# Selective-scan and attention kernel: directions joined without a drain, B and C rows loaded apart, first job's operands loaded a stretch ahead

## What is computed

```python
def step(h, xs_t):                       # over L = 2304 positions
    d_t, u_t, B_t, C_t = xs_t
    dA = jnp.exp(d_t[..., None] * A)     # 192 channels x 16 states
    h = h * dA + (d_t * u_t)[..., None] * B_t[:, :, None, :]
    y = jnp.einsum('bkdn,bkn->bkd', h, C_t)
    return (h, y)
...
xs = jnp.stack([x_hw, x_wh, x_hw[..., ::-1], x_wh[..., ::-1]], axis=1)   # 4 directions
delta = jax.nn.softplus(dts + dt_b[None, :, :, None])
...
ys = ys[:, 0:2] + ys[:, 2:4, :, ::-1]    # directions 0 and 2, 1 and 3 are added
```

## Time and profile before

| what | value |
|---|---|
| runs | 10106.07, 10117.13, 10135.11 us |
| profiled execution, span of the program on the core | 10102.8 us |
| median of the runs over that span | 14.3 us more |
| busy share of the span | PE 78%, DVE 72%, ACT 64%, POOL 60% |
| scans | 2304 (8 images x 288 steps) |
| DMA | 1534.77 MB, mean 152 GB/s |

### The profile page before, as it was taken

The page is one execution under the profiler, slowest core; times in us unless marked ns, Lnnn a source line. Parts: engine busy times, 40 slices in busy tenths (PEclk is TensorE's granted clock), DMA queues, the critical chain, the costliest instruction groups (busy, mean ns, idle before and its releaser), DMA issues.

```text
span 10102.8 us, 176447 instructions
## 1 busy us (share of the span) xinstructions
PE 7866.5 (78%) x54736; PEld 2569.1 (25%) x54736; DVE 7322.5 (72%) x6576; ACT 6466.3 (64%) x11830; POOL 6076.6 (60%) x4450
## 2 busy tenths in 40 slices
PE   5576668888788887888778887888878884888768
PEld 2122222222222232222322222222222221222212
DVE  1788848886688866888488875888668895889620
ACT  2343348775577746777477764877468783777578
POOL 0677627774477735777267763877448783777310
PEclk7565579897898978998788987988789995989789
DMA  2556525654356625565256552565345652565300
GB/s 62 165 182 196 182 72 185 190 187 126 123 187 186 186 86 165 186 187 175 74 185 191 186 162 87 187 192 181 113 137 187 193 184 79 187 189 181 109 27 20
DMA packets 767149, 1534.77 MB, mean 152 GB/s; under 512 B 85304, under 2 KB 411428, under 8 KB 757232
## 3 DMA queue, kind: packets, MB, share of 16 engines
q1 hardware_dynamic: 761584, 1520.71, 48.2%
q10 hardware_dynamic: 4608, 2.36, 0.1%
HBM read 1270.29 MB, written 252.44 MB: 151 GB/s over the span
## 4 chain that ended last, share of the span: by engine, by line
PE 37%; issue 19%; DVE 14%; ACT 11%; DMA 9%; POOL 5%; SPq 4%; ACTq 1%; DVEq 0%; POOLq 0%
PE ps L1896 7%; DMA job_u<-u_scratch 6%; PE ps L1828 6%; PE ps L1762 5%; PE ps L1816 5%; ACT probs_buf L1251 4%; DVE rings L1478 4%; DVE ps L1457 3%; DVE job_buf L1478 3%; POOL hc_buf L1016 2%; PE ps L1803 2%; PE ps L1845 1%; PE ps L2012 1%; ACT rings L1238 1%; PE ps L2011 1%
## 5 line engine op out<-in xcount | busy, mean ns | idle before, releaser
L1251 ACT ACTIVATE probs_buf<-ps 128x384 f32<-128x384 f32 x6912 | 3151.0, 491 | 1168.1 <-PE ps L1896 1102.9
L1016 POOL TENSOR_TENSOR hc_buf<-rings,rep 128x768 f32<-128x768 f32 x1152 | 2094.0, 1818 | 1220.6 <-DVE rings L1478 794.6
L1896 PE MATMUL ps<-qp_buf,kp_buf 108*128 108x384 bf16 x6912 | 2282.3, 351 | 616.4 <-ACT probs_buf L1251 283.2
L1016 POOL TENSOR_TENSOR hc_buf<-job_buf,rep 128x768 f32<-128x768 f32 x1152 | 2094.8, 1818 | 979.1 <-DVE job_buf L1478 970.1
L1457 DVE TENSOR_TENSOR ps<-ps,rep 128x768 f32<-128x768 f32 x2304 | 2175.9, 944 | 506.6 <-PE ps L1804 383.3
L1828 PE MATMUL ps<-probs_buf,v_buf 128*13 128x384 f32 x13824 | 1571.1, 529 | 75.0 <-DVE att_buf L1496 43.9
L1816 PE MATMUL ps<-hc_buf,sum_states 128*32 128x144 f32 x24576 | 1496.8, 331 | 145.0 <-POOL hc_buf L1016 111.3
L1803 PE MATMUL ps<-st_buf,pick_channel 96*128 96x512 bf16 x2304 | 1005.5, 436 | 588.4 <-DVE rings L1478 231.0
L1478 DVE TENSOR_TENSOR_SCAN job_buf<-rings,ps 128x768 f32<-128x768 f32 x768 | 1368.4, 1782 | 100.5 <-ACT rings L1238 55.2
L1896 PEld LDWEIGHTS ps<-qp_buf,kp_buf 108*128 108x128 bf16 x6912 | 648.5, 97 | 3087.2 <-ACT probs_buf L1251 2132.5
L1238 ACT ACTIVATE st_buf<-st_buf,a_cols 128x768 f32<-128x768 f32 x1152 | 1062.2, 927 | 88.0 <-DMA st_buf<-delta_scratch 87.8
(11 more groups left out here) (196 smaller groups left out, 7851.1 us busy)
## 6 DMA issues: line engine op xcount, KB each, us to landing
st_buf<-delta_scratch SPq DMA_DIRECT2D x1152, 384.0 KB
rings<-delta_scratch SPq DMA_DIRECT2D x1152, 384.0 KB
part_scratch<-job_buf SPq DMA_DIRECT2D x1152, 72.0 KB, 3.2
st_buf<-part_scratch SPq DMA_DIRECT2D x192, 432.0 KB, 6.9
rep<-xd_scratch SPq DMA_DIRECT2D x192, 384.0 KB
job_u<-u_scratch SPq DMA_DIRECT2D x192, 192.0 KB
delta_scratch<-job_buf SPq DMA_DIRECT2D x192, 192.0 KB, 4.8
qp_buf<-qk_scratch SPq DMA_DIRECT2D x864, 36.0 KB
```

The source lines that it names most:

```text
L1016: pool.tensor_tensor(hc[tile % 2][:, chunk(kk, v)], h_ring[t % 2], rep_third(1, kk, v), ALU.mult).then_inc(s["hc_ready"], 1)
L1251: act.activation(probs[(m % 2) * HG + h], bank(slots["score", p]), ACT.Exp, scale=SCALE)\
L1896: pe.matmul(bank(slots["score", p]), k_parts[:, h, m * 128:(m + 1) * 128], q_ring[:, (kk * NS + q) % 2, h, :], start=True, stop=True).then ...
```

## The change

Four things are changed.

1. The six sum parts and two evacuations at the end of a direction are taken into the next direction's first steps, where the same steps of any other stretch do them for the stretch before. This holds for the three joins of an image. The last direction still ends with them.
2. `y_stored` becomes one semaphore for each q. The y of stretch 5 is no longer stored in a row of 16 DMAs right after it, but over t = 5 to 8 of stretch 6. Direction 2 waits for `y_stored[q]` before it overwrites that part of `y_acc`, at t = 6 of each stretch.
3. Chunks 1 and 2 of B are loaded in steps 22 and 23 of the last stretch, as `b_ready` tells that DVE has finished with the old third. C chunk 1 is loaded in step 23, and C chunk 2 at t = 0 of the next direction.
4. `LOAD_JOB` is `(20, 2, 9)` and `JOB_START` is `(2, 7, 13)`. Job 0's operands are loaded at step 20 of the stretch before (`load_next_job`), across directions and images too.

```diff
-LOAD_JOB = (0, 5, 11)
-JOB_START = (4, 9, 15)
+LOAD_JOB = (20, 2, 9)
+JOB_START = (2, 7, 13)
...
+            def load_next_job(b, kk, q, more):
+
+                if q + 1 == NS:
+                    if kk + 1 == K and not more:
+                        return
+                    b, kk, q = (b, kk + 1, 0) if kk + 1 < K else (b + 1, 0, 0)
+                else:
+                    q = q + 1
+                if kk + 1 < K:
+                    load_job(b, b * K + kk + 1, KS_ORDER[kk + 1], q, 0)
+                elif more:
+                    load_job(b + 1, (b + 1) * K, KS_ORDER[0], q, 0)
...
-                    if prep and t in LOAD_JOB:
+                    if prep and t in LOAD_JOB[1:]:
                         load_job(nb, kidx + 1, nk, q, LOAD_JOB.index(t))
+                    if t == LOAD_JOB[0]:
+                        load_next_job(b, kk, q, more)
...
+                    if kk == 2 and q == 0 and 5 <= t < 9:
+                        sp.wait_ge(s["y_ev"], kidx * NT)
+                        store_y(1, NS - 1, 4 * (t - 5), 4 * (t - 4))
...
+                    if last and same and t in (BODY - 2, BODY - 1):
+
+                        c = t - (BODY - 3)
+                        sp.wait_ge(s["b_ready"], (kidx + 1) * DSTEPS - (SPT - c))
+                        load_rep(b, kk + 1, c, (0,))
+                    if last and same and t == BODY - 1:
+                        sp.wait_ge(s["hc_ready"], (kidx + 1) * DSTEPS - 2)
+                        load_rep(b, kk + 1, 1, (1,))
+                    if t == 0 and q == 0 and kk:
+                        sp.wait_ge(s["hc_ready"], kidx * DSTEPS - 1)
+                        load_rep(b, kk, 2, (1,))
...
                     load_st(kk + 1, 1)
-                    for c in range(1, SPT):
-
-                        sp.wait_ge(s["hc_ready"], (kidx + 1) * DSTEPS - (SPT - c))
-                        load_rep(b, kk + 1, c)
...
-                    if kk % 2:
-                        sp.wait_ge(s["y_ev"], (kidx + 1) * NT)
-                        store_y(kk, NS - 1, 0, 8 if kk + 1 == K else 16)
+                sp.wait_ge(s["y_ev"], (b + 1) * K * NT)
+                store_y(K - 1, NS - 1, 0, 8)
...
-                        if t % SPT == 0 and not (first and t < 2 * SPT):
-                            y_evacuate(kidx, q, t // SPT - 2, kk % 2,
-                                       ab if kk == 0 and first and t == 2 * SPT else None)
+                        if t % SPT == 0 and not (first and kk == 0 and t < 2 * SPT):
+                            T = t // SPT - 2
+                            if first and T < 0:
+
+                                y_evacuate(kidx - 1, NS - 1, T + 2 * TG, (kk - 1) % 2)
+                            else:
+                                y_evacuate(kidx, q, T, kk % 2,
+                                           ab if kk == 0 and first and t == 2 * SPT else None)
...
-                    for T in (2 * TG - 2, 2 * TG - 1):
-                        y_evacuate(kidx, NS - 1, T, kk % 2)
+                    if kk + 1 == K:
+                        for T in (2 * TG - 2, 2 * TG - 1):
+                            y_evacuate(kidx, NS - 1, T, kk % 2)
...
                     elif not first:
                         sum_tile(kidx, q - 1, T + 2 * TG, i)
+                    elif kk:
+                        sum_tile(kidx - 1, NS - 1, T + 2 * TG, i)
...
-                    for n in range(8 * TG - 6, 8 * TG):
-                        sum_tile(b * K + kk, NS - 1, n // 4, n % 4)
+                for n in range(8 * TG - 6, 8 * TG):
+                    sum_tile(b * K + K - 1, NS - 1, n // 4, n % 4)
```

27 lines of the change are left out of this document (15 added, 12 removed).

## The result

The changed kernel takes 10202.15 us, median of 4 runs (10191.0 to 10211.44); the kernel before, beside it on the same chip, 10119.25 (10106.07 to 10135.11). The ratio is 1.008, 95% interval 1.0066 to 1.0095. The change costs some 83 us, where the prediction had it gain 227. The profiled run took 10196.26 us with a span of 10194.5, against 10102.8 before.

A forecast was written before the change was run, and what follows sets the result against it. DVE was taken to set the pace wherever fed, starved at joins and by PE's late broadcasts. Gains 88 + 156 less 20 made 224 us off the 10102.8 span, forecast 9890 us, range 9730 to 10015.

The forecast's parts named there:

- the other loads of jobs: Earlier loads of job 1, and its softplus meeting the attention's projection on ACT: 0.25 us a stretch each, 20 us in all.
- the rest: Part of DVE's 38.9 us broadcast wait beyond late operands: mostly PE waiting for ACT to empty a bank; left alone.
- The rival slower: Job 1's operands, issued at t = 2 in the join's burst, arrive late and stop PE: 10170 us, chance 0.04.
- The rival *more: Join waits shrink to 1 us each and PE's faster clock cuts DVE's other waits: 9730 us, chance 0.23.
- The rival *less: Transfers are the new bound, loads served at no more than 190 GB/s: 10010 us, chance 0.18.
- Job 0's operands, 156 us: Loaded at step 20 of the stretch before, PE's 19.5 us of waits an image become DVE's gain: 156 us for eight.
- Joins, 88 us: Removing the drain at three joins: 16 of 27.1 us lost stay, 11 gained an image, 88 for eight.
- the transfers' way: Issue to landing of B and C thirds at joins: taken as 8, 10, 11 and 11 us.
- the upper bound of the text: Thirds at joins land at the slow end, 10.7 to 13 us: gain only 5 us an image, or 40.
- the cover of the `st_buf` load: Four steps or 11 us before a direction's first broadcast; costed at nothing, 1 to 3 us a join if gone.
- POOL waiting longer for `rep` than DVE did: Sign at the joins that the forecast is wrong: POOL's wait for B and C rows exceeds DVE's earlier one.
- stretches without such a wait above 72 us: Sign of a wrong forecast: stretches without waits for rows on POOL or at job 1's product stay above 72 us.

The follow-up runs named there:

- The leftovers alone: Changed kernel with the previous attention piece's last work (denominators, projection, residual) two steps later, starts still 2, 7, 13: 10143.09 us, ratio 1.0027.
- Both edits together: Changed kernel with that attention work two steps later and four unused matmuls at each job's start step: 10021.82 us, ratio 0.991.
- parts_early: Changed kernel with jobs at 4, 9, 15, last C third before the keys, job 1's parts stored and first `st_buf` group loaded earlier: 9962.95 us, ratio 0.9846.
- ahead_only: Kernel before with only job 0's operands loaded at step 20 of the stretch before, starts 4, 9, 15, drain kept: 10041.3 us, ratio 0.9921.
- join_only: Changed kernel without the load ahead, jobs at 4, 9, 15; joins, y stores and B and C loads kept: 10055.29 us, ratio 0.9939.

## Why the prediction was wrong, point by point

**The step that failed** is the one on "the other loads of jobs": 0.25 us a stretch, 20 us in all, for job 1's softplus beside the projection and its loads at t = 2. (At 0.25 us the 93 stretches that make jobs would make it 23.) No wait for the operands of jobs 1 and 2 shows in images 1 to 6, so the loads were rightly priced low. The shift costs 165 us, 1.8 us for each of the 93 stretches. It was sized as a meeting of two ACT instructions. What it does instead is put jobs 0 and 1 right ahead of the leftovers that take banks of the same ring, and all three where PE's wait for the relu is followed by the low clock. The prediction knew this wait, called it "the rest" beside the earlier trace rows, and said that the change leaves it alone. In length it does: 22.1 and 23.2 us. But a part of its price is in the matmuls behind it, and that part was there before, too: filling the wait gives 67 us (by the ratios) at the starts 4, 9, 15 and 111 at 2, 7, 13. The difference, 44 us, is an estimate of what the clock alone adds to the shift's cost (the two gains are of different versions). The leftovers alone make 54. Both edits together give 172, more than the 159 of the shift; less the 67 that the old starts have to gain as well, that accounts for some 105, and about 54 stay open, in the main at job 0.

The miss adds up. Against its forecast the shift cost 145 us more (165 for 20), job 0's operands gained 84 less (72 for 156), the joins 30 less (58 for 88), and joins and operands together 53 less than the two apart (77 for 130). That is 312 us; from a gain of 227 to a loss of 83 it is 310.

**The rival slower** had the right sign and nearly the size (10170) for a wrong reason: PE waited for job 1's operands at no step 7. The rival *more* had the clock, with the opposite sign: as a cost that falls when waits at the joins shrink. No rival moved the clock within a plain stretch. The rival *less* read the mean of the windows as 187 GB/s, where weighted by time it is 185.4 and one stretch moved 193. It took 190 GB/s as the most that the loads can be served at; that falls by one stretch of parts_early (stretch 4), which has no join and moves 204:

```profile
5285.72:5355.86 70.14, 61.44 (x533) 19.16 (x532) 65.51 (x58) 58.40 (x112) 59.01 (x45) 0.95 0.60 204
```

**Job 0's operands, 156 us.** The mechanism was right: the six waits are gone. The term was twice too large. Alone it gains 72 us by the medians (ahead_only; its profiled run was the slowest of its four, so that the table shows less). By the table the plain stretches gain 1.8 us, stretch 0 1.1 and those behind joins 9.5, and the joins give 7.1 back. DVE's wait for the broadcast did fall by 21.6 us of an image, so the step from PE's wait to DVE's held. What was put at nothing is what came after it: longer waits for the rows and the sums, and waits for the operands of jobs 1 and 2.

**Joins, 88 us.** Alone 58 (join_only), and not as reckoned. The drain did go: at join 2 of the changed kernel the last scan starts at 5557.27 and the next direction's first at 5560.08.

```profile
5557.27 1.81 DVE L1506 TENSOR_TENSOR_SCAN job_buf<-rings,ps 128x768 f32<-128x768 f32 x1
...
5560.08 1.75 DVE L1506 TENSOR_TENSOR_SCAN rings<-st_buf,ps 128x768 f32<-128x768 f32 x1
5567.58 0.97 DVE L1485 TENSOR_TENSOR ps<-ps,rep 128x768 f32<-128x768 f32 x1 [5.75 <-DMA rep<-xd_scratch]
...
5571.56 0.97 DVE L1485 TENSOR_TENSOR ps<-ps,rep 128x768 f32<-128x768 f32 x1 [0.84 <-DMA rep<-xd_scratch]
```

But the transfers' way was taken at 8 to 11 us. The first B third, issued at 5556.02, let DVE go on at 5567.58, 11.6 us later; the last C third, issued at 5567.68, let POOL go on at 5583.05, 15.4 us later. It was also issued 7.6 us behind the first scan, where 6.3 had been reckoned (0.8 and the keys' 5.50): keys (3.44 us) and one delta (3.12) stood ahead of it on SP. So the upper bound of the text (the C thirds cost nearly what the drain did) was the nearer one. The drain had lain largely in the shadow of these transfers. With starts at 4, 9, 15 the cover of the `st_buf` load was gone too, at 4.5 to 5.3 us a join, where I had said 1 to 3.

**What was right.** POOL waiting longer for `rep` than DVE did (40.6 against 12.2 us), and stretches without such a wait above 72 us, were named ahead as signs that the forecast fails, and both came. The scans across join 2 stand some 3 us apart, as said; but of the waits for `rep` behind it on DVE only one is short (0.84 us), and a long one (5.75) stands ahead of it. Stretch 0 stayed near its time in image 4 (86.32 against 88.81 us), though over images 1 to 6 it loses 2.8 us more.

The gains of join and load do not add: 72 and 58 make 77. That both end at the rows' landing is the likely reason, but it is argued, not shown. With the last C third and job 1's parts in their place they make 153 (parts_early, 9962.95, against the 10116.25 beside it).

## What to carry to other kernels

Price a move of work by the engine that waits behind it, at the clock that it then has. One wait of under 1 us cost 2.4 here, since PE ran the next two steps at its lower level; where PE has little slack, look at the granted clock of windows as short as one step before an edit that changes where PE waits, and try a few matmuls in the gap. When a wait is removed, ask what was done unseen beneath it: here a drain lay over transfers, and a wait for rows, it seems, over a job. And try two suspects together as well as one by one: at job 1, of 2.0 us that a stretch lost more, the leftovers' shift gave back 0.3 and the extra matmuls 0.8 by themselves, and 2.1 together.

## What the runs showed of the hardware

- After one wait of 0.96 us the granted clock stood at 0.58 and 0.59 in the next two steps, and a broadcast took 0.63 us instead of 0.38. With four matmuls of no use (1.06 us) in that wait it stayed at 1.00.
- Extra matmuls on a PE that is 79% busy made the kernel faster each of the three times they were tried: 10202.15 to 10075.24 us, 9962.95 to 9884.29, and 10143.09 to 10021.82.
- A `dma_start` of SP, 0.6 us elsewhere, took 3.12 us in the crowd behind join 2 (the delta at 5564.30): the issue itself took that long, and what stood behind it in SP's order came late.
